# GpSimd raises four numbers per partition to a power where it raised six

## What is computed

```python
m = jnp.mean(x, axis=axis, keepdims=True)
v = jnp.var(x, axis=axis, keepdims=True)
xf = (x - m) / jnp.sqrt(v + eps)                       # second layer norm
xn = xf / jnp.maximum(jnp.linalg.norm(xf, axis=-1, keepdims=True), 1e-12)
group_scores = xn @ _l2norm(group_centroids).T
expert_scores = xn @ _l2norm(expert_centroids).T + bias
```

## Time and profile before

| what | us |
|---|---|
| median of 3 runs | 600.62 |
| the three runs | 596.67, 600.62, 604.53 |
| the profiled execution, whole | 604.68 |
| its span, first to last instruction | 602.5 |
| attention steps with the change in them, about | 60 to 320 |
| expert stage, first transposes to last products, about | 347 to 559 |

### The profile page before, as it was taken

One profiled execution on the slowest core, in us unless ns is written; L12 is line 12 of the kernel. 1 busy time (PEld: TensorE's weight loads), 2 busy tenths in 40 slices (PEclk: granted clock), 3 DMA queues, 4 the chain that ended last, 5 costly groups with the idle time before them and its releaser, 6 DMA issues.

```text
span 602.5 us, 20827 instructions
## 1 busy us (share of the span) xinstructions
PE 513.2 (85%) x7427; PEld 423.3 (70%) x7427; DVE 424.7 (70%) x1297; ACT 323.1 (54%) x832; POOL 343.0 (57%) x362
## 2 busy tenths in 40 slices
PE   3558997989988798887669889999989999999756
PEld 2336665766666566665545589999989999998544
DVE  5666799779999899966676366756666676664264
ACT  3336775767777677655546225455446555454200
POOL 8520113276666566655777507777777777777600
PEclk9659998989999999977899979999999999999977
DMA  7889998887877665520000134543534554541198
GB/s 254 234 234 249 250 248 235 225 268 212 240 231 208 210 209 151 137 66 25 21 12 10 36 99 140 150 123 108 164 119 140 171 155 149 170 118 49 24 394 292
DMA packets 79417, 98.33 MB, mean 163 GB/s; under 512 B 12097, under 2 KB 59999, under 8 KB 79216
## 3 DMA queue, kind: packets, MB, share of 16 engines
q1 hardware_dynamic: 65280, 82.92, 47.2%
q0 software_dynamic: 9216, 12.02, 6.4%
q10 hardware_dynamic: 4848, 2.40, 1.4%
HBM read 50.00 MB, written 54.30 MB: 173 GB/s over the span
## 4 chain that ended last, share of the span: by engine, by line
PE 38%; DVE 6%; DMA 5%; issue 4%; POOL 3%; ACT 2%; SPq 0%; POOLq 0%; DVEq 0%; ACTq 0%
PE banks L1115 18%; PE banks L1141 12%; DMA rload<-pair_results 3%; PE banks L1126 3%; POOL expert_slots L490 2%; DVE mx L1239 1%; PE banks L932 1%; DMA pair_results<-yout,yidx 1%; PE banks L1050 1%; POOL pair_results L618 1%; PE banks L1167 0%; DMA xg<-expert_slots 0%; SPq L440 0%; PE banks L874 0%; ACT yout L805 0%
## 5 line engine op out<-in xcount | busy, mean ns | idle before, releaser
L618 POOL DMA_INDIRECT pair_results<-yout,yidx x160 | 159.3, 996 | 67.0 <-issue 38.1
L490 POOL DMA_INDIRECT expert_slots<-xfe,sidx x128 | 127.8, 998 | 89.7 <-issue 38.9
L1115 PE MATMUL banks<-xgT_parts,wgu_parts 128*128 128x320 f32 x768 | 131.3, 320 | 1.9 <-DVE hact L1506 1.7
L1115 PEld LDWEIGHTS banks<-xgT_parts,wgu_parts 128*128 128x128 f32 x768 | 113.9, 190 | 4.6 <-DVE hact L1506 2.3
L1239 DVE TENSOR_REDUCE mx<-banks 128x8 f32<-128x1024 f32 x64 | 78.0, 1219 | 21.0 <-PE banks L882 21.0
L1506 DVE TENSOR_TENSOR hact<-hact,banks 128x320 f32<-128x320 f32 x128 | 56.6, 482 | 43.0 <-ACT hact L786 42.1
L805 ACT ACTIVATE yout<-banks,ypair 128x128 f32<-128x128 f32 x160 | 44.8, 372 | 76.2 <-PE banks L1141 73.8
L655 ACT ACTIVATE pt<-banks 128x512 f32<-128x512 f32 x128 | 69.3, 593 | 27.9 <-PE banks L913 26.6
L1141 PE MATMUL banks<-wdn,hact 128*128 128x128 f32 x640 | 76.6, 275 | 1.1 <-DVE hact L1506 1.1
L1141 PEld LDWEIGHTS banks<-wdn,hact 128*128 128x128 f32 x640 | 75.0, 192 | 1.3 <-issue 1.3
L786 ACT ACTIVATE hact<-banks 128x320 f32<-128x320 f32 x128 | 53.5, 452 | 33.1 <-PE banks L1115 31.4
(11 more groups left out here) (154 smaller groups left out, 945.5 us busy)
## 6 DMA issues: line engine op xcount, KB each, us to landing
expert_slots<-xg SPq DMA_DIRECT2D x32, 325.0 KB, 4.8
xg<-expert_slots SPq DMA_DIRECT2D x32, 325.0 KB
pair_results<-zero SPq DMA_DIRECT2D x32, 256.0 KB
rload<-pair_results SPq DMA_DIRECT2D x16, 512.0 KB, 8.9
kS<-rotated_keys SPq DMA_DIRECT2D x32, 240.0 KB
qS<-rotated_queries SPq DMA_DIRECT2D x32, 192.0 KB
wgu<-in_L_ffn_wg_dram SPq DMA_DIRECT2D x32, 128.0 KB
wgu<-in_L_ffn_wu_dram SPq DMA_DIRECT2D x32, 128.0 KB
```

The source lines that it names most:

```text
L490: g.indirect_dma_start(out=slots_d, out_offset=bass.IndirectOffsetOnAxis(ap=sidx[:, m % NB, j, k:k + 1], axis=0), in_=xfe[:, m % NB, j, k, ...
L618: g.indirect_dma_start(out=pairs_d, out_offset=bass.IndirectOffsetOnAxis(ap=yidx[:, c, j:j + 1], axis=0), in_=yout[:, c, j, :], in_offset= ...
L1115: last = mm(bank[2 + 2 * w + h][:, 0:CH], wgu_parts[:, e.b, wp, w, h * P:(h + 1) * P], xgT_parts[:, e.b, xp, ch * CH:(ch + 1) * CH], start ...
```

## The change

Both kernels need (v + eps) to the power -1/2 and the inverse length. The second was (v + eps) to the power 1/2 times (D v) to the power -1/2; now it is one power, (D v / (v + eps)) to the power -1/2. The quotient is made by VectorE: v + eps once, D v into a new tile `energy`, the reciprocal of v + eps, and their product into `pin`. The product `unit` goes, and so does its semaphore. The marks of the experts are added up by VectorE in both.

```diff
-            g.memset(powers[:, 0], -0.5).then_inc(S.powers_set, 1)
-            g.memset(powers[:, 1], 0.5).then_inc(S.powers_set, 1)
-            g.memset(powers[:, 2], -0.5).then_inc(S.powers_set, 1)
+            g.memset(powers[:, :, :], -0.5).then_inc(S.powers_set, 1)
...
                 def lengths_raised():
-                    pool.wait_ge(S.ln2, 6 * w + 6)
+                    pool.wait_ge(S.ln2, 8 * w + 8)
...
-                    wait(pool, S.unit_ready, w - 1)
+                    wait(pool, S.sc_ready, w - 1)
                     g.tensor_tensor(pout[:, w % 2], pin[:, :, :], powers[:, :, :], ALU.pow).then_inc(S.w_pow, 1)
...
                 def lengths():
...
-                    v.tensor_scalar(pin[:, 0:2], var.unsqueeze(1).broadcast_to([P, 2, 2]), EPS, None, ALU.add).then_inc(S.ln2, 1)
-                    v.tensor_scalar(pin[:, 2], var, float(D), 1e-24 * EPS, ALU.mult, ALU.max).then_inc(S.ln2, 1)
+                    v.tensor_scalar(pin[:, 0], var, EPS, None, ALU.add).then_inc(S.ln2, 1)
+                    v.tensor_scalar(energy[:, 0], var, float(D), 1e-24 * EPS, ALU.mult, ALU.max).then_inc(S.ln2, 1)
+                    dve.wait_ge(S.ln2, 8 * w + 5)
+                    v.reciprocal(energy[:, 1], pin[:, 0]).then_inc(S.ln2, 1)
+                    dve.wait_ge(S.ln2, 8 * w + 7)
+                    v.tensor_tensor(pin[:, 1], energy[:, 0], energy[:, 1], ALU.mult).then_inc(S.ln2, 1)
                 def second_norm():
...
-                    v.tensor_tensor(unit[:, :], pout[:, r % 2, 1], pout[:, r % 2, 2], ALU.mult).then_inc(S.unit_ready, 1)
 
                 def scores():
                     dve.wait_ge(S.router_done, r + 1)
-                    dve.wait_ge(S.unit_ready, r + 1)
+                    dve.wait_ge(S.w_pow, r + 1)
                     v.tensor_tensor(sc[:, :, :], bank[5][:, PW:PW + 2 * (NGR + NE)].rearrange("p (j e) -> p j e", j=2),
-                                    unit[:, :].unsqueeze(2).broadcast_to([P, 2, NGR + NE]), ALU.mult)\
+                                    pout[:, r % 2, 1].unsqueeze(2).broadcast_to([P, 2, NGR + NE]), ALU.mult)\
```

More of the change, by code:

```diff
@@ L181, in block_kernel @@
         mhalf = sb("mhalf", [P, 8])
-        powers = sb("powers", [P, 3, 2])
+        powers = sb("powers", [P, 2, 2])
         st1 = sb("st1", [P, NT, 6])
@@ L190, in block_kernel @@
         off1 = sb("off1", [P, NT])
-        pin = sb("pin", [P, 3, 2])
-        pout = sb("pout", [P, 2, 3, 2])
+        pin = sb("pin", [P, 2, 2])
+        energy = sb("energy", [P, 2, 2])
+        pout = sb("pout", [P, 2, 2, 2])
         off2 = sb("off2", [P, 2])
-        unit = sb("unit", [P, 2])
         xn = sb("xn", [P, 2, D])
@@ L261, in block_kernel @@
         qk_written v_done v_evac v_prev vals_zero p1_scores p1_reduced negm mT_done mT_evac
-        p2_scores exp_done pv_done pv_evac pvT_done recip onorm oT_done oT_evac wout_done x1_ready ln2 powers_set w_pow off2_ready unit_ready xf_ready xf_copied
+        p2_scores exp_done pv_done pv_evac pvT_done recip onorm oT_done oT_evac wout_done x1_ready ln2 powers_set w_pow off2_ready xf_ready xf_copied
         xfT_done xfT_evac router_done sc_ready route gate_exp gate_done marks_added sel_ready acc_ready pos_done
@@ L531, in lengths_raised @@
                 def lengths_raised():
-                    pool.wait_ge(S.ln2, 6 * w + 6)
+                    pool.wait_ge(S.ln2, 8 * w + 8)
                     if w == 0:
-                        pool.wait_ge(S.powers_set, 3)
+                        pool.wait_ge(S.powers_set, 1)
                     wait(pool, S.xf_ready, 2 * (w - 1))
-                    wait(pool, S.unit_ready, w - 1)
+                    wait(pool, S.sc_ready, w - 1)
                     g.tensor_tensor(pout[:, w % 2], pin[:, :, :], powers[:, :, :], ALU.pow).then_inc(S.w_pow, 1)
@@ L1311, in second_stats @@
                     for j in range(2):
-                        dve.wait_ge(S.ln2, 6 * w + 1 + j)
+                        dve.wait_ge(S.ln2, 8 * w + 1 + j)
                         hold(dve)
@@ L1316, in lengths @@
                     var = mv2[:, w % 2, :, 1]
-                    dve.wait_ge(S.ln2, 6 * w + 4)
+                    dve.wait_ge(S.ln2, 8 * w + 4)
                     wait(dve, S.w_pow, w)
-                    v.tensor_scalar(pin[:, 0:2], var.unsqueeze(1).broadcast_to([P, 2, 2]), EPS, None, ALU.add).then_inc(S.ln2, 1)
-                    v.tensor_scalar(pin[:, 2], var, float(D), 1e-24 * EPS, ALU.mult, ALU.max).then_inc(S.ln2, 1)
+                    v.tensor_scalar(pin[:, 0], var, EPS, None, ALU.add).then_inc(S.ln2, 1)
[4 more added lines that the diff above has]
+                    v.tensor_tensor(pin[:, 1], energy[:, 0], energy[:, 1], ALU.mult).then_inc(S.ln2, 1)
                 def second_norm():
```

## The result

The changed kernel takes 604.64 us (median of 22 runs, 599.92 to 610.44), the kernel before in the same series 601.34 (22 runs, 596.67 to 606.86): ratio 1.0053, 95% interval 1.0029 to 1.0078. That is 3.2 us more (1.7 to 4.7): under the 2% that counts as a difference, and near the 2.1 us forecast. The profiled execution of the changed kernel took 610.44 us, the slowest of the 22, so what follows compares pieces of its trace with the same pieces of the trace before, not the two spans.

The account below looks back on a forecast made before the run. VectorE was taken to bound the full steps. Terms -0.42 (w = 3), +3.2 (`lengths`), -0.63 (`unit`), -0.35 (power, w = 14) and +0.32 (`lengths`, w = 15) gave +2.1 us: 602.7 us, range 597.5 to 607.5.

Parts of the forecast that it names:

- What bounds the kernel: Attention steps: VectorE bounds the full steps, busy 15.04 of 15.82 us; POOL is not the bound.
- Rival B: Full steps: PE is as good as the bound and hides the longer `lengths`; -0.7 us, 599.9 us; chance 0.16.
- `lengths`, +0.32 a step: VectorE, `pin` to `sc`: 0.46 us in place of 0.14, so 0.32 more; +3.2 us over ten steps.
- Rival C: VectorE's `lengths`: the waits are free, +0.07 us in ten steps, -0.35 twice; 600.6 us; chance 0.10.
- Rival D: VectorE's `lengths`: two new self-waits a step released 0.4 us late, +12.8 us, above 615.5 us; chance 0.04.
- Absorbed up to w = 3: w = 0 to 2 and `lengths` of w = 3: VectorE's delay is hidden by the slots' fill, 0 us.
- The power in a full step, worth nothing: POOL, full steps: the power is 0.35 us shorter, but its reader `off` comes later, so nothing is gained.
- The two places, w = 3 and w = 14: The powers of w = 3 and w = 14 count, being undisturbed: -0.35 us each.
- The sum: Whole kernel: -0.42 + 3.2 - 0.63 - 0.35 + 0.32 = +2.1 us, giving 602.7 us.
- A: The forecast itself: VectorE's 0.32 us lies on the path in ten steps; 602.7 us; chance 0.68.
- A step that was wrong: POOL's power: claimed about 1.0 us undisturbed and 1.4 beside a long VectorE instruction.

Follow-up runs that it names:

- the chain of eight: Changed kernel plus eight unused two-number reciprocals behind `lengths` in all 16 blocks, each waiting for the one ahead: 622.95 us, ratio 1.0307 to the kernel before.
- the chain in the first four blocks: Changed kernel plus eight unused reciprocals behind `lengths`, each waiting for the one ahead, only for w < 4: 603.26 us, ratio 0.9984 to the kernel before.
- the reordered kernel: Changed kernel with the same VectorE instructions reordered so independent ones fill the waits of `lengths`: 597.67 us, then 598.9 us again; weighted mean ratio 0.9927 to before.

## Why the prediction was right, step by step

**What bounds the kernel.** VectorE in the full steps, said the prediction. The step grew by 0.29 where `lengths` grew by 0.34 and `unit`'s 0.07 went; it grew by 0.55 to 0.6 with eight free reciprocals more, did not shrink with the smaller power alone, and shrank when VectorE's gaps were filled. Rival B (PE takes up the addition) falls with the same numbers. It was close to true further on: with the chain of eight, VectorE did begin to wait for PE.

**`lengths`, +0.32 a step.** Measured +0.34, with the intervals named ahead (0.20, 0.19, 0.07: 0.20, 0.20, 0.08). The pair of the earlier trace rows carried it. The step was forecast at +0.25 and came to +0.29 or +0.30, since `lengths` costs 0.02 more and the rest of the step, where `unit`'s 0.07 was to go, is only 0.04 or 0.05 shorter.

**Rival C, the waits are free.** It would have given 0.07 a step. The two chains of eight settle it: 0.06 without the waits, 0.20 with them. The Trainium skill, VectorE: DVE Perf Modes, "Rules for kernel authors", advises to count operations and not semaphores; for instructions on two numbers per partition these runs disagree, and the measurement decides. Rival D (waits released 0.4 us late) would have shown idle time in front of the new instructions; a chain of eight in each of 16 blocks shows no more than the 0.03 us from one instruction's end to the next one's start, and its waits cost 0.14 each (0.20 less 0.06).

**Absorbed up to w = 3.** Right in what it costs, and the chain in the first four blocks shows it; in that profile it was mostly VectorE's waits for PE that took it up. In the changed kernel POOL's dispatch that waits for the fill of the slots stands where it stood. Timeline of POOL, then of VectorE, in the changed kernel; they answer to the earlier trace rows:

```profile
121.92 1.16 POOL L488 DMA_INDIRECT expert_slots<-xfe,sidx  x1 [5.46 <-DMA expert_slots<-xg]
...
124.38 1.06 POOL L535 TENSOR_TENSOR pout<-pin,powers 128x4 f32<-128x4 f32 x1
```

```profile
125.47 0.16 DVE L1326 SCALAR_TENSOR_TENSOR off<-mv,pout 128x2 f32<-128x2 f32 x1 [1.47 <-POOL pout L535]
```

The power took 0.30 less, and VectorE went on 0.53 earlier (forecast 0.35), 0.23 of it because the power started earlier, behind a fill that landed earlier. VectorE waited for the power for 1.47 us where it was 2.21.

**The power in a full step, worth nothing.** Right: twelve numbers in place of four leave the step as it was. The two places, w = 3 and w = 14, are less sure. With twelve numbers, 1.6 us more (-0.8 to 4.0) and 1.7 (-0.3 to 3.8) leave room for the forecast's term (2.3 and 1.9) and for none; VectorE waits for the power at both places in the profile that the forecast was read from, but nowhere in six of the 14. In the changed kernel it waits at w = 3 alone: at w = 14 the power ends at 304.45, while VectorE is at its own marks until 305.30. The term itself was 0.30 and not 0.35, nearer to the straight line's 0.29. The smaller power alone, 2.7 us less in place of 0.7, is outside the forecast.

**The sum.** +2.1 forecast, +3.2 (1.7 to 4.7) measured. The part that can be read from the trace is larger by the step's 0.04 or 0.05 in nine steps, 0.4 us. The rest is within the interval. The time alone could not have told A from B and C, whose times all lie in the range; the full steps and the two chains of eight do. The two profiled spans differ by 5.8 us, and that is not the change's price. The first product of the expert stage starts at 354.85 us where it started at 351.05, 3.8 later in place of some 2. Up to w = 4 the changed kernel is 0.7 ahead. From w = 4 to w = 13 it takes 151.87 us where it took 148.29; nine steps at 0.29 make 2.6 of the 3.6, and one wait of 1.12 us about the rest:

```profile
250.44 1.23 DVE L1237 TENSOR_REDUCE mx<-banks 128x8 f32<-128x1024 f32 x1 [1.12 <-issue]
```

Waits of 0.9 to 1.4 us for PE stand in front of the maxima of the same step in three other profiles, one of them, with 1.02 us, of the kernel before with twelve numbers; so such a wait also comes without the longer `lengths`. From w = 13 to w = 15 it takes 25.89 us where it took 24.98, and 25.39 in the second profile of the kernel before; the forecast's terms there cancel, 0.32 for `lengths` of w = 13 and -0.35 for the power of w = 14, a gain that did not come. From the first load of the expert stage to the first load of the results it takes 231.1 us where it took 229.1, and between 226.5 and 231.4 in the 14 profiles, whatever was changed. A span is to be split by stage before its difference is explained.

**A step that was wrong.** "The power takes about 1.0 us undisturbed and 1.4 beside a long VectorE instruction": in the changed kernel it took 1.06 us in a full step too, where it had taken 1.81. It cost nothing here, and the last section says why.

## What to carry to other kernels

On an engine that paces a step, price a short instruction by the distance of starts in the trace, and its wait for the one ahead apart from it: 0.06 to 0.08 us without, 0.20 with, for two numbers per partition. An identity that saves work on an engine with slack and adds a dependent chain on the one that paces costs the chain; putting independent instructions into the chain's gaps turned the same change from +3.2 us into -4.4 (with the power as long as before, from +3.3 into 0.2). Ask of every engine's saving whether its reader was waiting for it: here that was so at two places of 16 at most, and in six of the 14 profiles at none.

## What the runs showed of the hardware that was not expected

**The order of starts decides who is slowed.** VectorE's product `parts` reads two long rows of 512 numbers. Timelines of POOL and of VectorE in the changed kernel:

```profile
185.95 1.06 POOL L535 TENSOR_TENSOR pout<-pin,powers 128x4 f32<-128x4 f32 x1
```

```profile
186.21 0.68 DVE L1289 TENSOR_TENSOR parts<-r,parts 128x512 bf16<-128x512 f32 x1
```

The product starts during the power, and neither is longer than alone. Before, the same product started at 185.64, ahead of the power at 185.74:

```profile
185.64 0.68 DVE L1291 TENSOR_TENSOR parts<-r,parts 128x512 bf16<-128x512 f32 x1
```

and the power took 1.81 in place of 1.36. In the reordered kernel the power of this step starts at 185.56, behind the product at 185.37, and takes 1.40. So in these steps the power is slowed only where the product has started first. Over all 14 profiles the same holds, with one exception. Every power that starts during a product is longer by what is left of the product, less about 0.14 us: 0.45 with 0.59 left at 185.74, 0.20 with 0.34 left at 138.51 in the kernel before. No power is longer by more than 0.05 where the product starts 0.1 us or more behind it. Where the product starts less than 0.1 behind, four powers of eight are slowed all the same, one of them in the changed kernel at w = 2, in the timelines of POOL and of VectorE:

```profile
101.37 1.64 POOL L535 TENSOR_TENSOR pout<-pin,powers 128x4 f32<-128x4 f32 x1
```

```profile
101.44 0.68 DVE L1289 TENSOR_TENSOR parts<-r,parts 128x512 bf16<-128x512 f32 x1
```

The product takes 0.66 to 0.69 us in all but four of its 224 instances, and at most 0.74.

**What a power costs by its size.** Undisturbed, with the numbers per partition: 0.77 us for two, 1.06 for four, 1.36 for six, 2.32 for twelve, which is about 0.15 us a number above 0.45 (an estimate from these four).
